# Building h in PSUM: the condition and the shared product seeded by ScalarE, the other products accumulated onto it

## What is computed

```python
# x (32, 64, 1024), cond (32, 128), conv weight (64, 16, 9) in 4 groups
h = conv1d(x, weight, padding=4, groups=4) + (cond @ c_weight.T)[:, :, None] + bias[None, :, None]
q = h @ Wq.T                               # 16 wide
scores = q @ keys.T                        # 64 experts
gate = softmax over the 16 largest scores, 0 elsewhere
z = (h @ A.T).reshape(..., 64, 8) * gate[..., None]
out = x + 2.0 * z.reshape(..., 512) @ B.T  # B is (1024, 512)
```

## Time and profile before

| | us |
|---|---|
| median of 3 runs | 233.9 (233.74 to 234.32) |
| span of the profiled execution, first to last instruction | 232.5 |
| TensorE matmul busy | 228.6 (98%) |
| TensorE weight loads busy | 203.9 (88%) |
| VectorE busy | 194.1 (83%) |
| ScalarE busy | 98.8 (43%) |

### The profile page before, as it was taken

How to read it: one execution, slowest core, us unless ns; L and a number is a source line. 1 busy time by engine, 2 the same in 40 slices (tenths; PEclk the granted TensorE clock), 3 DMA queues, 4 the chain that set the end, 5 groups by cost and what they waited for, 6 DMA issues and landing times.

```text
span 232.5 us, 4022 instructions
## 1 busy us (share of the span) xinstructions
PE 228.6 (98%) x1381; PEld 203.9 (88%) x1381; DVE 194.1 (83%) x469; ACT 98.8 (43%) x245; POOL 7.5 (3%) x16
## 2 busy tenths in 40 slices
PE   8999999999999999999999999999999999999995
PEld 7989998798989989898898989889898989898885
DVE  1799889999999899998989989898998979847232
ACT  4897758256252353525425362432526242101100
POOL 2010062000000000000000000000000000000000
DMA  6999055742633728164471826448282343553632
GB/s 197 375 402 395 25 151 166 265 145 93 204 146 86 246 74 270 67 186 150 97 251 58 253 96 167 154 106 254 66 261 84 58 170 90 186 161 111 178 139 92
DMA packets 23781, 38.79 MB, mean 167 GB/s; under 512 B 2768, under 2 KB 11856, under 8 KB 23760
## 3 DMA queue, kind: packets, MB, share of 16 engines
q1 hardware_dynamic: 23616, 38.45, 51.2%
q10 hardware_dynamic: 144, 0.08, 0.3%
HBM read 25.94 MB, written 12.58 MB: 166 GB/s over the span
## 4 chain that ended last, share of the span: by engine, by line
PE 97%; DMA 1%; DVE 0%; issue 0%
PE p_z L676 38%; PE p_out L714 13%; PE p_out L715 13%; PE p_out L722 13%; PE p_conv L630 10%; PE p_conv L574 5%; PE p_out L676 3%; DMA sm<-in_small 1%; PE p_out L574 1%; PE p_z L698 1%; PE p_t L582 1%; PE p_z L582 0%; PE p_z L722 0%; PE p_z L714 0%; PE p_z L715 0%; PE p_t L688 0%
## 5 line engine op out<-in xcount | busy, mean ns | idle before, releaser
L714 PE MATMUL p_out<-b_hi,zt_hi 128*128 128x512 f32 (+1 forms) x128 | 50.1, 392 | 0.0
L715 PE MATMUL p_out<-b_hi,zt_lo 128*128 128x512 f32 (+1 forms) x128 | 50.1, 392 | 0.0
L676 PE MATMUL p_z<-a_hi,h_hi 128*128 128x264 f32 x240 | 34.3, 286 | 0.1
L722 PE MATMUL p_out<-b_lo,zt_hi 128*128 128x512 f32 (+1 forms) x128 | 34.4, 391 | 0.0
L676 PE MATMUL p_z<-a_hi,h_lo 128*128 128x264 f32 x240 | 34.2, 285 | 0.0
L676 PE MATMUL p_z<-a_lo,h_hi 128*128 128x264 f32 x240 | 33.9, 284 | 0.0
L676 PEld LDWEIGHTS p_z<-a_hi,h_hi 128*128 128x128 f32 x240 | 32.0, 188 | 1.9 <-issue 0.5
L676 PEld LDWEIGHTS p_z<-a_hi,h_lo 128*128 128x128 f32 x240 | 31.3, 188 | 0.0
L676 PEld LDWEIGHTS p_z<-a_lo,h_hi 128*128 128x128 f32 x240 | 31.1, 188 | 0.0
L390 ACT ACTIVATE h_hi<-h_t 128x1024 fp32r<-128x1024 f32 x16 | 17.1, 1068 | 28.1 <-DVE h_t L838 28.0
L715 PEld LDWEIGHTS p_out<-b_hi,zt_lo 128*128 128x128 f32 x128 | 24.0, 188 | 5.6
(11 more groups left out here) (108 smaller groups left out, 264.6 us busy)
## 6 DMA issues: line engine op xcount, KB each, us to landing
x_nat<-in_x_rows SPq DMA_DIRECT2D x16, 512.0 KB, 4.9
out_dram<-x_nat SPq DMA_DIRECT2D x31, 256.0 KB, 3.2
x_blk<-in_x_blocks SPq DMA_DIRECT2D x14, 516.0 KB, 4.3
z_dram<-a_raw SPq DMA_DIRECT2D x64, 64.0 KB, 1.8
a_raw<-z_dram SPq DMA_DIRECT2D x16, 256.0 KB, 3.6
a_raw<-in_a_wq SPq DMA_DIRECT2D x8, 264.0 KB, 6.8
x_nat<-in_b_w SPq DMA_DIRECT2D x4, 512.0 KB, 9.2
x_blk<-in_x_blocks SPq DMA_DIRECT2D x2, 258.0 KB, 3.9
```

Source lines behind the costliest of these rows:

```text
L676: mm = nc.tensor.matmul(z_bank(t, b)[:, 0:HB], h[:, t % 2, r, :], a[:, r, b * HB:(b + 1) * HB], start=k == 0 and r == 0, stop=k == 2 and r ...
L714: nc.tensor.matmul(dst, zt_hi[:, t % 2, c, :], b_hi[:, c, cols], start=c == 0, stop=False)
L715: nc.tensor.matmul(dst, zt_lo[:, t % 2, c, :], b_hi[:, c, cols], start=False, stop=False)
L722: mm = nc.tensor.matmul(dst, zt_hi[:, t % 2, c, :], b_lo[:, c, start:stop], start=False, stop=c == JC - 1)
```

## The change

`conv_s`, `add_shared` and `s_hw` are gone. `conv_sum` now writes bank 1 of `p_conv`. ScalarE's pass reads each sample's 64 shared values there, adds the condition, and writes them twice, back into bank 1 and into bank 0 (8 ACTIVATEs of 128 columns, PSUM to PSUM). `conv_pair` accumulates its products onto what lies there (the first matmul of a bank no longer starts a new sum). `turn_h` reads the two banks of `p_conv` itself. `conv_pair(i+2)` stands one `out_part` later on TensorE and waits for ScalarE's pass; ScalarE makes the pass before `exp(i)` and `split_z(i-1)` and no longer after them; VectorE does `split_z(i-1)` behind `turn_h`.

```diff
         def rows_done(t, ab=1):
             if t == 0:
                 return s_hc, ab + 1
-            return (s_hc, t + 2) if t < TW else (s_hw, 2 * (t - TW) + ab + 1)
+            return (s_hc, t + 2) if t < TW else (s_conv, 2 * t + ab + 1)
...
                 if t > TW:
-                    act.wait_ge(s_hw, 2 * (t - TW))
+                    act.wait_ge(s_tr, 2 * (t - 1) + 1)
+                both = p_conv[:, 0:2, :].rearrange("q ab (k n) -> q ab k n", n=NN)
                 for n in range(NN):
                     at = t % TG * NN + n
-                    last = nc.scalar.activation(conv_s[:, n, :], p_conv[:, 2, :].rearrange("q (k n) -> q k n", n=NN)[:, :, n],
+                    last = nc.scalar.activation(both[:, :, :, n], both[:, 1, :, n].unsqueeze(1).to_broadcast([P, 2, LK]),
                                                 ACT.Identity, bias=u[:, t // TG, at:at + 1])
                 last.then_inc(s_cu, 1)
...
-                if 3 < i < NT - 2:
-                    split_z(i - 1)
-                exp(i)
-                if i >= NT - 2:
-                    split_z(i - 1)
                 if i + 2 < NT:
                     add_u_shared(i + 2)
-                if i == 3:
-                    split_z(2)
+                exp(i)
+                split_z(i - 1)
...
-            def conv_products(t, dst, ws, part):
+            def conv_products(t, dst, ws, part, onto):
...
-                    mm = nc.tensor.matmul(dst, w, x[:, t % 2, part * XO:(part + 1) * XO], start=k == 0, stop=k == 2)
+                    mm = nc.tensor.matmul(dst, w, x[:, t % 2, part * XO:(part + 1) * XO], start=k == 0 and not onto,
+                                          stop=k == 2, skip_group_check=onto)
...
-                if t > TW:
-                    pe.wait_ge(s_cu, t - TW)
-                conv_products(t, p_conv[:, 2, :], (ws_hi[:, g % 2, :], ws_lo[:, g % 2, :]), 0).then_inc(s_cs, 1)
+                if t == TW:
+                    pe.wait_ge(*rows_done(t - 1))
+                else:
+                    pe.wait_ge(s_tr, 2 * t)
+                conv_products(t, p_conv[:, 1, :], (ws_hi[:, g % 2, :], ws_lo[:, g % 2, :]), 0, False).then_inc(s_cs, 1)
 
             def conv_pair(t):
                 g = t // TG
+                pe.wait_ge(s_cu, t - TW + 1)
                 for ab in range(2):
-                    pe.wait_ge(*rows_done(t - 1, ab))
                     conv_products(t, p_conv[:, ab, :], (w_hi[:, g % 2, ab, :], w_lo[:, g % 2, ab, :]),
-                                  1 + ab).then_inc(s_conv, 1)
+                                  1 + ab, True).then_inc(s_conv, 1)
...
                 scores(i)
-                if i + 2 < NT:
-                    conv_pair(i + 2)
-
-
                 if i >= NT - 2:
                     out_part(i - 3, 1)
                 if i < NT - 1:
                     out_part(i - 2, 0)
+                if i + 2 < NT:
+                    conv_pair(i + 2)
                 if i < NT - 3:
                     out_part(i - 2, 1)
...
-                    src = h_c[:, t % 2, :, part * LK:(part + 1) * LK]
-                nc.vector.transpose(dst, src.rearrange("q n (k c) -> q n k c", c=CI)).then_inc(s_tr, 1)
+                    if t < TW:
+                        src = h_c[:, t % 2, :, part * LK:(part + 1) * LK].rearrange("q n (k c) -> q n k c", c=CI)
+                    else:
+                        src = p_conv[:, part].rearrange("q (k c n) -> q n k c", n=NN, c=CI)
+                nc.vector.transpose(dst, src).then_inc(s_tr, 1)
```

More of the change, by code:

```diff
@@ L83, in adaln_ffn @@
         ws_lo = sb("ws_lo", [P, 2, P], F32R)
-        conv_s = sb("conv_s", [P, NN, LK])
         h_c = sb("h_c", [P, 2, NN, LB])
@@ L157, in adaln_ffn @@
         s_cu = sem("s_cu")
-        s_hw = sem("s_hw")
         s_conv = sem("s_conv")
@@ L816, in differ @@
                                         blocks[:, XE:XS], ALU.subtract).then_inc(s_xd, 1)
[L818 to L823, removed]
             def turn_h(t, part):
@@ L833, in turn_h @@
                     half = slice(part * NH, (part + 1) * NH)
-                    dst, src = h_rows[:, half], h_c[:, 0, half, :]
+                    dst, src = h_rows[:, half], h_c[:, 0, half, :].rearrange("q n (k c) -> q n k c", c=CI)
                 else:
                     dst = h_rows[:, :, part * R // 2:(part + 1) * R // 2, :]
-                    src = h_c[:, t % 2, :, part * LK:(part + 1) * LK]
-                nc.vector.transpose(dst, src.rearrange("q n (k c) -> q n k c", c=CI)).then_inc(s_tr, 1)
+                    if t < TW:
[3 more added lines that the diff above has]
+                nc.vector.transpose(dst, src).then_inc(s_tr, 1)
             def split_h(t):
@@ L1036, in _ @@
                 take_first(i)
-                if 3 < i < NT - 3:
-                    split_z(i - 1)
                 if i < NT - 3:
@@ L1045, in _ @@
                 gate(i)
-                if i + 2 < NT:
-                    add_shared(i + 2, 0)
                 turn_z(i)
@@ L1050, in _ @@
                     add(i - 3, 1)
-                    split_z(i - 1)
                 if i + 2 < NT:
-                    add_shared(i + 2, 1)
                     turn_h(i + 2, 0)
                     turn_h(i + 2, 1)
+                split_z(i - 1)
                 if i == 3:
-                    split_z(2)
                     split_keys()
```

## The result

The changed kernel takes 234.45 us (median of 12 runs, 234.18 to 235.01) against 233.92 for the kernel before (12 runs): ratio 1.0022, 95% interval 1.0012 to 1.0032. It is 0.5 us slower, which is less than the 0.7 us that I had set as the limit of what can be told, but with twelve runs a side it stands clear of zero.

What follows compares the result with a forecast made beforehand. TensorE's matmuls were taken as the bound, busy 228.6 of 232.5 us. Four terms of 0 each left the span at 232.5 us and the timed forecast at 233.9, own range 233.3 to 234.6, full range 233.2 to 236.2.

Steps and rivals of the forecast that it cites:

- TensorE as the bound, no gap to win: Steps 3 to 13: TensorE waits for nobody, each step is as long as its matmuls, no gap to win back.
- Part 1: TensorE's work: same number and shapes of matmuls, only reordered, accumulating onto PSUM at the same pace; cost 0.
- Part 2: Hand-over TensorE to ScalarE to TensorE, eleven times: pass 2.18 us, slack 0.22 us, up to 0.34 with load's reserve; cost 0.
- Part 3: Work behind ScalarE's pass: `exp` later but VectorE doesn't wait; in step 13 the gate slips 0.45 us, just fits; cost 0.
- Part 4: VectorE: additions of 14.7 us busy time go, `turn_h` transposes from PSUM at 0.68 us; all off the path, cost 0.
- B: VectorE becomes late by slow PSUM transposes or L917 waiting: up to 0.5 us, 234.4; chance 0.02 for over 0.7 us.
- A: ScalarE's pass lasts 2.6 to 3.0 us, so TensorE's weight load waits eleven times: 235 to 236, up to 240.5; chance 0.18.
- C: TensorE's matmuls quicken with less VectorE traffic: 0.3 us in all, 233.6; chance 0.05 for this or unseen gain over 0.7.

Runs made afterwards that it cites:

- The first: The changed kernel with `add(0, 0)` moved ahead of `split_h(4)` in VectorE's list; 234.05 us against 234.01, ratio 0.9998.
- the second experiment: The kernel before, with `conv_pair(5)` placed behind `out_part(1, 0)` in step 3 alone; 234.38 us against 234.01, ratio 1.0028.

## Why the prediction was wrong, point by point

The forecast was no change, 233.9 us; measured were 234.45, inside the range of 233.2 to 236.2, but slower and clear of the noise. That it lies inside even the narrow range of 233.3 to 234.6 is luck: no term of the sum held this wait.

- **TensorE as the bound, no gap to win: right.** Its waits and the length of a step say so in all kernels, and no variant here was measurably faster than the kernel before.
- **Part 1, another order of the same matmuls, cost 0: wrong, and this is the whole error.** I gave the cost of the pair moving back and looked at what the pair waits for. I did not look at what the out product waits for when it moves forward by 1.4 us. The order listing in front of the prediction shows it, `[waits s_added,s_ztlo,s_zthi]`. I had also said that the other steps look like the one in the timeline, and worked out step 9 alone. In step 9 the `add` ends 6 us before the out product asks for it; step 3 follows the start-up, where VectorE's list puts a split of 1.2 us ahead of it. The step that failed should have read: in step 3, 0.5 us, once. The first and the second experiment show it from both sides.
- **Part 2, the hand-over: right in mechanism and size.** Pass 2.15 us against 2.18; slack 0.27 against 0.22 (136.16 + 0.06 to 136.49); nothing shows. The load's reserve is 0.12 to 0.13, where I had up to 0.12. Writing PSUM in place of SBUF hardly changed what counts, the pace: a pass of eight takes 2.15 us in place of 2.18. The figure of 2.44 us that I worked out from the Trainium skill ("ScalarE: Activation LUTs", What ACT_TABLE_LOAD costs) was 0.29 too long.
- **Part 3, step 13 just fits: right in outcome, by less than I had reckoned.** The gate slipped by 0.58 us and not by 0.45; 0.12 of that is the time from the end of `exp` to L907 (190.97 to 191.09), which I had left out. L907 waited 0.61 us for `exp`. The weight load of `z_product(14)` comes 0.10 us later after `conv_sum` than before (4.88 against 4.78), its reserve takes that up, and the distance to the end stayed 40.74. The added ACTIVATEs show that this place has no slack at all, while the middle steps have 0.4 us. I had also priced the slip for `z_product(14)` alone and not for the query of `scores(14)`.
- **Part 4, VectorE's relief is worth nothing: right for the sum, not in every step.** `turn_h` out of PSUM costs 0.676 us, as taken. VectorE's busy time fell by 11.7 us and not by about 15, because I had added up rows that overlap. In step 13 the relief keeps away a loss of 0.5 us, behind the later gate; I had set both to 0.
- **The rivals.** B didn't happen, though its time, 234.4, agrees by accident: the transposes kept their pace, L907 waited in step 13 alone, and what TensorE waited for was an `add` that had not moved. A didn't happen; the slope that I gave it is right (0.53 us per step for 0.51 us of pass, once the cover is used up). C didn't happen either. The one that did happen, a transfer of cover from one product to another, was not on the list.

## What to carry to other kernels

When work is put in another order on the engine that bounds, price both sides: what the piece that moves back is waited for by, and what the piece that moves forward waits for itself. Do it for the first and the last step of a loop and not for a middle one only; here the middle steps had room for every part of the change, the first lost 0.5 us, and the last would have lost 0.5 us too without the time that VectorE had gained. And if a change frees an engine that is off the path, ask which cover it uses up on the one that is on it: this one gave VectorE 1.2 us per tile, of which only step 13 had any use, and left TensorE with a slack of 0.3 to 0.4 us.

## What the runs showed of the hardware

- An ACTIVATE of 128 columns out of PSUM with a bias per partition has the same pace into PSUM as into SBUF, 0.25 us from start to start, also where it writes the bank that it reads (eight take 2.15 us in the changed kernel, 2.18 into SBUF in the kernel before). The mean length printed for one is 355 ns against 399 in the same profile.
- The hand-over from ScalarE's last ACTIVATE to a weight load that waits for it took 0.05 us, in all eleven steps of each run with two or four more ACTIVATEs.
- Behind a matmul of 512 columns a weight load that came 0.12 us late cost 0.01 at most; one that came 0.23 late cost 0.10, one that came 0.75 late 0.63.
- Eleven waits of TensorE's weight load of 2.4 us each, with the matmuls idle for 2.1 to 2.2 us, cost 35 us and not 26: in six of the eleven steps the granted clock fell to 0.50 for over 3 us behind the wait, in the other five it stayed at 1.000. In the run with `exp` first nine idle times of 1.0 us, one in each of the steps 4 to 12, and one of 1.6 us in step 3 left it at 1.000.
